# Attention kernel: value products and row-maximum products take turns in three PSUM banks, and the row-maximum products move behind the scores

## The reference

```python
xs = jnp.reshape(gn(x), (B, T, C))              # B 16, T 1024, C 512
q, k, v = (jnp.einsum('btc,hcd->bhtd', xs, W) for W in (Wq, Wk, Wv))
scores = jnp.einsum('bhtd,bhsd->bhts', q, k) / sqrt(64)
out = jnp.einsum('bhts,bhsd->bhtd', softmax(scores), v)
y = x + reshape(transpose(out) @ Wproj + bproj)
```

## Time and profile before

| | |
|---|---|
| median of 3 runs | 4859.68 us (4859.32 to 4861.87) |
| the profiled execution | 4860.69 us, its span 4858.9 us |
| mean granted TensorE clock | 0.997 |
| busy: PE, weight load, DVE, ACT, POOL | 95%, 72%, 57%, 59%, 48% |

### The profile page before, as it was taken

The page is one execution under the profiler, slowest core; times in us unless marked ns, Lnnn a source line. Parts: engine busy times, 40 slices in busy tenths (PEclk is TensorE's granted clock), DMA queues, the critical chain, the costliest instruction groups (busy, mean ns, idle before and its releaser), DMA issues.

```text
span 4858.9 us, 72553 instructions
## 1 busy us (share of the span) xinstructions
PE 4610.2 (95%) x20352; PEld 3496.1 (72%) x20352; DVE 2775.0 (57%) x5284; ACT 2864.6 (59%) x5507; POOL 2319.6 (48%) x1837
## 2 busy tenths in 40 slices
PE   7999999999999999999999999999999999999998
PEld 5777777777777776767767677676776767767675
DVE  5655646556465564655656556465564656646454
ACT  4665746556465564655646566465664746647464
POOL 2444545445454454544545445454544545445455
PEclk9999999999999999999999999999999999999999
DMA  2111111111111111111111111211112111121101
GB/s 70 35 38 56 31 54 36 45 48 32 54 35 50 45 35 53 33 50 43 35 55 36 51 43 30 64 29 54 37 30 63 36 51 34 33 61 36 54 23 52
DMA packets 156933, 212.69 MB, mean 44 GB/s; under 512 B 56544, under 2 KB 57568, under 8 KB 156512
## 3 DMA queue, kind: packets, MB, share of 16 engines
q1 hardware_dynamic: 156512, 207.47, 15.4%
HBM read 105.12 MB, written 34.08 MB: 29 GB/s over the span
## 4 chain that ended last, share of the span: by engine, by line
issue 50%; POOL 42%; PE 6%; POOLq 1%; ACT 1%; DVE 1%; DMA 0%; SPq 0%; ACTq 0%; DVEq 0%
POOL prob_l L999 32%; POOL o L1016 6%; POOL res L1022 3%; PE bank L486 1%; PE bank L529 1%; POOL rstd L991 1%; POOLq L998 1%; PE bank L546 1%; PE bank L658 1%; PE bank L660 1%; PE bank L659 1%; PE bank L540 0%; PE bank L539 0%; POOLq L1015 0%; ACT prob_h L678 0%
## 5 line engine op out<-in xcount | busy, mean ns | idle before, releaser
L999 POOL TENSOR_TENSOR prob_l<-prob,prob_h 128x512 fp32r<-128x512 f32 x1408 | 1797.3, 1288 | 2389.4 <-ACT prob_h L678 2379.4
L678 ACT ACTIVATE prob<-bank 128x512 f32<-128x512 f32 x2048 | 1237.8, 604 | 1633.6 <-PE bank L540 1487.7
L832 DVE TENSOR_REDUCE smax<-bank 128x1 f32<-128x512 f32 x2048 | 1348.7, 684 | 954.8 <-PE bank L546 942.6
L678 ACT ACTIVATE prob_h<-bank 128x512 fp32r<-128x512 f32 x2048 | 1237.2, 604 | 194.3 <-PE bank L660 154.5
L658 PE MATMUL bank<-prob_h,vh 128*128 128x512 f32 x2048 | 832.6, 407 | 109.0 <-ACT acc L749 99.1
L546 PE MATMUL bank<-k_hl,q_hh 128*128 128x512 f32 x2048 | 798.9, 434 | 33.5 <-DVE smax L832 30.6
L539 PE MATMUL bank<-q_hh,k_hl 128*128 128x512 f32 x2048 | 822.6, 402 | 3.0 <-issue 2.1
L540 PE MATMUL bank<-q_lm,k_h 65*128 65x512 f32 x2048 | 812.3, 397 | 0.0
L659 PE MATMUL bank<-prob_h,vl 128*128 128x512 f32 x2048 | 808.0, 395 | 0.0
L660 PE MATMUL bank<-prob_l,vh 128*128 128x512 f32 x2048 | 807.9, 394 | 0.0
L771 DVE TENSOR_TENSOR prob_l<-prob,prob_h 128x512 fp32r<-128x512 f32 x640 | 507.4, 803 | 501.8 <-ACT prob_h L678 501.7
(11 more groups left out here) (58 smaller groups left out, 4360.1 us busy)
## 6 DMA issues: line engine op xcount, KB each, us to landing
xs<-in_x SPq DMA_DIRECT2D x128, 256.0 KB, 2.8
q_hh<-q_hh SPq DMA_DIRECT2D x256, 128.0 KB, 2.2
k_hl<-k_h SPq DMA_DIRECT2D x256, 128.0 KB, 2.4
inv_b<-inv_dram SPq DMA_DIRECT2D x256, 128.0 KB, 2.8
res<-in_x SPq DMA_DIRECT2D x128, 256.0 KB, 2.7
out_x<-res SPq DMA_DIRECT2D x128, 256.0 KB, 2.0
q_lm<-q_lm SPq DMA_DIRECT2D x256, 2.0 KB
den<-acc SPq DMA_DIRECT2D x256, 2.0 KB, 1.7
```

Source lines behind the costliest of these rows:

```text
L678: return nc.scalar.activation(out, ps[ST + bank][:, :], ACT.Exp, scale=SCALE)
L832: nc.vector.tensor_reduce(smax[:, j:j + 1], ps[SM + j % 2][:, :], AX.X, ALU.max).then_inc(rows_used, 1)
L999: nc.gpsimd.tensor_tensor(prob_l[:, r3, :], prob[:, ring2, :], prob_h[:, r3, :].bitcast(F32), ALU.subtract).then_inc(prob_l_pool, 1)
```

## The change

There is no bank of its own for the value products and no pair for the row maxima any more. Banks 3, 4 and 5 are shared. The value product of each half takes the bank that `VALUE_BANK` names, so that two halves in a row never have the same one; the row-maximum products go to whichever of the other two was used longest ago. `turns` works this out for each step, with the earlier user of the bank for each new one, and `turn_free` waits for that user: a maximum taken, a copy done, or, for the first user in a step, all 16 maxima of the step before. In the last product of block 7 or 15 the bank that the next half's value product will take is left out.

The row-maximum products also move from the end of `other_work` to a place right behind the scores of the block (in blocks 0 and 8: right behind the value product), and VectorE takes them in the same block instead of the next (in blocks 0 and 8 behind `prob_l`).

```diff
-ST, SM, PVB, WB = 0, 3, 5, 6
+ST, TURN, WB = 0, 3, 6
+VALUE_BANK = (0, 1, 2, 0, 1, 2, 0, 1, 2, 0, 1, 2, 0, 1, 2, 1)
...
+def turns(h, per_slot):
+    user = [None, None, None]
+    row_turn, value_turn = [], []
+    age = {b: -1 for b in range(3)}
+    user[VALUE_BANK[2 * h - 1]] = ("value", -1)
+    for i in range(BLOCKS):
+        tc, t = divmod(i, 8)
+        value, after = VALUE_BANK[2 * h + tc], VALUE_BANK[(2 * h + tc + 1) % BLOCKS]
+        if t == 0:
+            value_turn.append(user[value])
+            user[value] = ("value", tc)
+            if tc:
+                age[VALUE_BANK[2 * h]] = 2 * i
+        for n in range(per_slot[i], 0, -1):
+            late = t == 7 and n == 1
+            bank = min((b for b in range(3) if b != value and not (late and b == after)),
+                       key=lambda b: (t != 7 or b != after, age[b]))
+            row_turn.append((bank, user[bank]))
+            user[bank] = ("row", len(row_turn) - 1)
+            age[bank] = 2 * i + 3 - n
+    return row_turn, value_turn
...
+        def turn_free(eng, s, user):
+            if user is None:
+                eng.wait_ge(rows_used, s.heads(BLOCKS, 1))
+            elif user[0] == "row":
+                eng.wait_ge(rows_used, s.heads(BLOCKS, 1, user[1] + 1))
+            elif not (s.section == "first" and user[1] < 0):
+                eng.wait_ge(acc_ready, s.heads(2, 0, user[1] + 1))
...
-                    pe.wait_ge(rows_used, s.heads(BLOCKS, 1, j - 1))
-                    row_scores((s.k + 1) % 2, j)
+                    bank, user = s.row_turn[j]
+                    turn_free(pe, s, user)
+                    row_scores((s.k + 1) % 2, j, bank)
...
+                    if i % TT:
+                        row_work(s, i)
                     if i in s.first[0]:
                         other_work(s, i)
...
-                    if t == 0 and not (first and tc == 0):
-                        pe.wait_ge(acc_ready, s.heads(2, 0, tc))
+                    if t == 0:
+                        turn_free(pe, s, s.value_turn[tc])
...
-                    bank = PVB
+                    bank = TURN + VALUE_BANK[2 * s.h + tc]
...
+                    if i % TT == 0:
+                        row_work(s, i)
                     if i not in s.first[0]:
                         other_work(s, i)
...
                     def maxima():
                         nonlocal hj
-                        for _ in range(per_slot[i - 1] if i else 0):
-                            take_max(hj, s.heads(BLOCKS, 1, hj + 1))
+                        for _ in range(per_slot[i]):
+                            take_max(hj, s.heads(BLOCKS, 1, hj + 1), s.row_turn[hj][0])
...
-                    if i not in s.first[1]:
+                    if i % TT and i not in s.first[1]:
                         maxima()
...
-                    if i in s.first[1]:
+                    if i % TT == 0 or i in s.first[1]:
                         maxima()
```

More of the change, by code:

```diff
@@ L161, in __init__ @@
         self.looped = section == "body"
+        self.row_turn, self.value_turn = turns(
+            self.h, max_blocks(self.h, self.has_next, self.looped and k == 8))
     def at(self, per_batch, const):
@@ L541, in scores, with row_scores @@
                                  start=False, stop=True).then_inc(scores_ready, 1)
-            def row_scores(slot, j):
+            def row_scores(slot, j, turn):
                 t, half = divmod(j, 2)
-                nc.tensor.matmul(ps[SM + j % 2][:, :], q_hh[:, slot, t * P:(t + 1) * P],
+                nc.tensor.matmul(ps[TURN + turn][:, :], q_hh[:, slot, t * P:(t + 1) * P],
                                  k_hl[:, slot, half * 512:(half + 1) * 512], start=True, stop=True).then_inc(rows_ready, 1)
@@ L581, in _ @@
                     pe.wait_ge(rows_used, j - 1)
-                row_scores(0, j)
+                row_scores(0, j, j % 2)
                 if j == 9:
@@ L612, in other_work, with row_work @@
                     entry(kind, a, lo, hi, bk, before, (s.h + (2 if kind == "qn" else 1)) % NH, wait)
+            def row_work(s, i):
                 per_slot = max_blocks(s.h, s.has_next, s.section == "body" and s.k == 8)
@@ L748, in copy_out @@
                     act.wait_ge(o_ready, s.heads(2, 0, tc - 1))
-                nc.scalar.copy(acc[:, tc, :], ps[PVB][:, :]).then_inc(acc_ready, 1)
+                nc.scalar.copy(acc[:, tc, :], ps[TURN + VALUE_BANK[2 * s.h + tc]][:, :]).then_inc(acc_ready, 1)
             def take_in_step(s, kind, a):
@@ L828, in take, with take_max @@
                     last.then_inc(taken[bank], 1)
-            def take_max(j, count):
+            def take_max(j, count, turn):
                 dve.wait_ge(rows_ready, count)
-                nc.vector.tensor_reduce(smax[:, j:j + 1], ps[SM + j % 2][:, :], AX.X, ALU.max).then_inc(rows_used, 1)
+                nc.vector.tensor_reduce(smax[:, j:j + 1], ps[TURN + turn][:, :], AX.X, ALU.max).then_inc(rows_used, 1)
             def combine(half, used):
@@ L876, in _ @@
                     for j in range(10, BLOCKS):
-                        take_max(j, j + 1)
+                        take_max(j, j + 1, j % 2)
                     combine(1, BLOCKS)
```

## The result

The changed kernel takes 5015.1 us (median of 4 runs, 5011.7 to 5020.4) beside 4859.5 for the kernel before; the ratio is 1.032, with a 95% interval of 1.0302 to 1.0338. I forecast 4780. The time went 155 us up instead of 80 down, outside the range, on the side that had a chance of 0.06. Of all executions here one, of e7_short_o, ran at a mean granted clock of 0.758 and took 5663 us; without it the median of that kernel moves by 0.8 us.

What follows compares the result with a forecast made beforehand. TensorE, in flight 95%, bounds the kernel; its copy and row waits cap the gain at 178 us. Head terms sum to 5.08 us a pass, times 15.5 is 79, plus 1 for clock: 4860 − 80 = 4780 us; 8-in-10 range 4705 to 4832.

Steps and rivals of the forecast that it cites:

- The value product of a new half hardly waits: Head boundaries: the copy (0.6 us) leaves TensorE's path; value products waiting for `acc` fall to none or a few us.
- the row maxima of the last step are in time for block 0: Into heads 2 and 3: the last two maxima end at 1942.2, exactly when TensorE arrives (1942.21).
- GpSimd's `prob_l` is the next obstacle in block 1 of head 5: Heads 4 to 5: TensorE arrives at 2040.27 but waits for it until 2040.83; a gain of 0.6, not 1.46.
- The projection's wait for `res` takes row products in: Projection step: row products can stand inside `proj` 5's wait for `res` (17.8 us in 15 waits), +0.46 a pass.
- Block 8 and the row products: Part on mid-head: +0.4 in heads 1 and 2, −0.77 in 4 and 5, −0.53 in 6, +0.46 in the projection step.
- No DMA is moved: Whole kernel: the moved instructions cost nothing themselves; SP's and POOL's queues keep their order.
- the rule of the prediction: TensorE's waits: each costs its printed idle plus 0.27 us (0.17 not printed, 0.10 restart).
- block 9: Plain heads: second row product waits 1.2 us for block 8's maximum behind `prob_l` (1.23); net −0.77 in heads 4 and 5.
- TensorE's waits for `spread` slightly longer: Profile after: the variance matmul's waits for `spread` grow slightly; no size given.
- The clock: Granted clock of 0.97 over 59 us behind the longest boundary wait; 1 us of gain counted for all such.
- The wait changes its cause rather than going: Head 7 to projection step: the 1.8 us boundary wait passes to POOL's `prob_l`, gaining only +0.35.
- Rival C: Slower: blocks with two row products hold value products behind untaken maxima; 558 lose 0.2 each, 112 us, 4892; chance 0.06.

Runs made afterwards that it cites:

- e7_short_o: Changed kernel with GpSimd's `o` of the second half made on 32 of 512 columns, part of the output left out: 4922.8 us.
- e8_old_split: Kernel before with the old order up to block 10 and the new from 11, old banks kept: 4953.7 us.
- e6_split: Kernel before with the three shared banks, old order up to block 10 and new from 11: 4905.2 us.
- e11_start3: Changed kernel with no row products before block 3, their numbers moved to blocks 3 to 7: 4957.3 us.
- e3_first: Changed kernel with row products behind the value product, maxima behind `prob_l`, in each head's first block that has any: 4960.3 us.
- e4_nine: Changed kernel with row products of blocks 9 and 10 behind the value product and taken behind `prob_l`: 4953.3 us.
- e5_both: Changed kernel with the edits of e3_first and e4_nine together: 4934.0 us.
- e18_before_norm10: Kernel before with GpSimd and VectorE exchanging the `prob_l` of blocks 9 and 10 in heads 3 to 5: 4859.0 us.

## Why the prediction was wrong, step by step

**Right.** The value product of a new half hardly waits: no wait for `acc` is left, and the row maxima of the last step are in time for block 0 (0.6 us in 4 printed waits in all; in head 5 they hold it 0.3 us, too short to be printed as a rule). GpSimd's `prob_l` is the next obstacle in block 1 of head 5, 0.3 us. The projection's wait for `res` takes row products in (17.8 to 5.8 us; I had +0.46 a pass, and 12 / 15.5 is 0.8). And e8_old_split against e6_split shows what the banks are worth when the order is the same: 48 us.

**The step that failed** stands under "Block 8 and the row products" as "No DMA is moved". It is true and misses the point: the consumer of a DMA was moved. I worked out block 0 by what the value product needs and never asked what the first row product needs when it comes a value product and `other_work` earlier, at a boundary whose wait I had just removed. The wait for `acc` was also the cover of the `k_hl` landing. The rows were there to see, a landing at 1980.15 and a product at 1980.62. Priced: 105 us of waits by the rule of the prediction, 97 by the starts of the matmuls, and the clock behind them. e11_start3, which has hardly any wait for the DMA, gets 58 back, and e3_first, which keeps the one in head 3, gets 55.

**Mis-sized, in the same direction: block 9.** The mechanism was right (a maximum held behind VectorE's `prob_l`, held by GpSimd's `o`) and so was the place. I took 1.23 us for that `prob_l` from its row. In the kernel before it starts 0.60 behind `o`; after, 0.15, and takes 1.67. A duration under contention is not a constant of the operation: it depends on when the two start, and the change moved one of them. By the gaps between the matmuls' starts the wait is then 1.5 us in heads 4 and 5, where I had 1.2, and 1.4 in head 6, and heads 1 and 2, where I had nothing, lose 0.95 each in block 10. Maxima cost 98 us more by the starts (107 by the rule of the prediction) where I had them about level; e4_nine gets 62 back.

**"TensorE's waits for `spread` slightly longer"** was 14.9 to 36.7 us. It is the same kind of meeting, in head 3, where VectorE's small products of 0.16 us end only with the GpSimd operation that they meet. I had looked for what reaches TensorE late, and not for what meets whom on the way.

**The clock** was in my sum with 1 us, and as a gain. The removed waits were replaced by others, up to 2.7 us long. All 43 stretches at the low clock stand right behind a wait of 1.2 us or more. The clock makes about 67 us of the loss by the starts of the matmuls. No run takes the clock away alone, so this share is read from rows and not an experiment.

**"The wait changes its cause rather than going"** was said of the boundary before the projection step, and was right, but the cause is the DMA (1.4 us) and not GpSimd's `prob_l`.

**Rival C** had the sign and the size of the row waits, but not the mechanism: it had the two-product blocks lose a little each. They don't; a few blocks lose 0.5 to 2 us each, where VectorE is held by GpSimd or a transfer is late.

**What stays open.** The costs of the edits are not additive (e5_both), so the shares above are those of the waits and not of independent causes. The new order makes 93 and 117 us in the old banks; the waits for `acc` (99.1 to 162.0 and 173.1 us) and the copy that starts 0.43 us later show the way, but no run takes this chain by itself. Why the clock falls behind 14 waits of one kernel and 3 of the same waits of another was not tried.

## What to carry to other kernels

When a wait is removed, ask not only who is late next at that place, but what the wait was covering: every DMA and every small operation that lands within it. When an instruction is moved earlier, list all its inputs, not only the buffer that it writes. And try an order head by head (or stage by stage): the same change took 1.8 us from one head of a pass and added 4.3 to another, and the version that beats both kernels keeps the new order only where it pays.

## What the runs showed of the hardware

A VectorE product of two SBUF operands that starts while a large GpSimd product runs can take up to 2.4 times its undisturbed time when it is large (0.69 to 1.67 us) and 8 times when it is small (0.16 to 1.27). The small one ends with GpSimd's (0.02 us behind it, in all 30 `dev` products and all 15 `spread` products that met one in the changed kernel). The large one ends about 0.55 us behind GpSimd's, whenever it started (the 100 `prob_l` of the changed kernel that started with 0.6 us or more of an `o` left). A product with one operand in PSUM (`dev` of L832) stays at 0.15 us beside the same work, and reductions from PSUM keep their mean of 684 ns over all 2048.

In a stream that keeps TensorE 93% busy, waits of 1.2 to 2.7 us were followed by stretches at the lower clock, 1.6 us lost in each: the wait printed as 1.84 us cost 3.7 in all (2.0 to the start, 0.1 at the next, 1.6 at the low clock). Of the 72 waits of 1.0 to 1.5 us in the changed kernel 14 were followed by such a stretch, of the 30 longer ones 29. The same 15 waits of 1.8 us were followed by 3 stretches in the kernel before and by 14 in e18_before_norm10.
